# First group's 32 maxima and first row made inside the projections; the last batch's routing moved into the attention's first steps

## What is computed

```python
qkv = (x @ W_qkv + b_qkv).reshape(B, T, 3, H, Dh)          # 16 heads of 16
q, k = rope(q), rope(k)
attn = softmax(einsum('bhqd,bhkd->bhqk', q, k) / 4)         # 1024 x 1024 for each of 64 heads
out = einsum('bhqk,bhkd->bhqd', attn, v) @ W_out + b_out
scores = sigmoid(x @ w_gate.T)                              # 16 experts in 4 groups
# the 2 best groups by the sum of their two best scores, in them the 4 best experts,
# their scores normalised to weights; a shared gated network of 256 beside them
routed = einsum('tef,ehf,te->th', silu(x@w1_e) * (x@w3_e), w2_e, combine)
```

## Time and profile before

| | us |
|---|---|
| median of 3 runs | 1216.02 |
| profiled execution, span from first to last instruction | 1217.1 |
| PE busy | 1150.2 (95%) |
| DVE busy | 959.9 (79%) |
| ACT busy | 750.6 (62%) |
| POOL busy | 578.9 (48%) |
| L1048, maximum on DVE, x512 | 1.222 each |
| L1022, exponential on ACT, x1024 | 0.596 each |
| stage A | 0 to 158.7 |
| prologue of stage B | 158.7 to 198.4 |
| attention's steps | 198.4 to 845 |
| stages C and D | 845 to 1217 |

### The profile page before, as it was taken

How to read it: one execution, slowest core, us unless ns; L and a number is a source line. 1 busy time by engine, 2 the same in 40 slices (tenths; PEclk the granted TensorE clock), 3 DMA queues, 4 the chain that set the end, 5 groups by cost and what they waited for, 6 DMA issues and landing times. The chain is left out here.

```text
span 1217.1 us, 27786 instructions
## 1 busy us (share of the span) xinstructions
PE 1150.2 (95%) x8310; PEld 582.5 (48%) x8311; DVE 959.9 (79%) x1451; ACT 750.6 (62%) x1568; POOL 578.9 (48%) x861
## 2 busy tenths in 40 slices
PE   4999767999999999999999999998999999998998
PEld 2555422333333333333333333333788887875665
DVE  6575685999999999999999999970555555556888
ACT  3666303888888888888888888887333333330000
POOL 6999947354465653232322323231576666661000
PEclk9999955999999999999999999999999999999999
DMA  6466743454435453343324332402777666655765
GB/s 221 156 202 216 224 110 140 180 163 125 126 106 145 125 143 86 87 109 96 94 80 117 89 95 79 103 29 64 215 225 228 205 204 213 194 165 185 234 220 173
DMA packets 127288, 181.74 MB, mean 149 GB/s; under 512 B 41441, under 2 KB 88929, under 8 KB 125282
## 3 DMA queue, kind: packets, MB, share of 16 engines
q1 hardware_dynamic: 111842, 138.55, 39.6%
q0 software_dynamic: 15360, 42.04, 10.0%
HBM read 99.71 MB, written 80.81 MB: 148 GB/s over the span
## 5 line engine op out<-in xcount | busy, mean ns | idle before, releaser
L1048 DVE TENSOR_REDUCE mx<-pm 128x1 f32<-128x1024 f32 x512 | 620.6, 1222 | 31.4 <-PE pm L1098 30.6
L1022 ACT ACTIVATE pr<-pst 128x512 f32<-128x512 f32 x1024 | 556.6, 596 | 86.3 <-PE pst L1109 34.9
L1098 PE MATMUL pm<-kt,qt 48*128 48x512 f32 x1024 | 386.6, 461 | 13.4 <-DMA qt<-s_q 8.0
L1109 PE MATMUL pst<-qt,kt 50*128 50x512 f32 x1024 | 377.7, 449 | 6.5 <-DMA qt<-s_m 6.5
L1121 PE MATMUL po<-pr,vt 128*17 128x256 f32 x4096 | 322.9, 388 | 9.9 <-ACT osb L1032 9.6
L1098 PEld LDWEIGHTS pm<-kt,qt 48*128 48x128 f32 x1024 | 157.1, 192 | 237.5 <-DVE mx L1048 173.1
L1274 POOL DMA_INDIRECT s_y<-ys_c,slot_c x144 | 139.6, 969 | 85.7 <-issue 46.4
L1121 PEld LDWEIGHTS po<-pr,vt 128*17 128x17 f32 x4096 | 69.0, 95 | 198.9 <-issue 110.3
L1109 PEld LDWEIGHTS pst<-qt,kt 50*128 50x128 f32 x1024 | 152.8, 186 | 18.8 <-ACT pr L1022 10.9
L950 POOL DMA_INDIRECT s_xg<-p_rows,p_slot x128 | 125.2, 978 | 56.0 <-issue 29.8
L1354 PE MATMUL pd<-w13s,xt_c 128*128 x576 | 149.5, 382 | 0.4 <-ACT xt_c L1284 0.4
(11 more groups left out here) (188 smaller groups left out, 1169.5 us busy)
## 6 DMA issues: line engine op xcount, KB each, us to landing
xg<-s_xg SPq DMA_DIRECT2D x144, 128.5 KB
yg<-s_y SPq DMA_DIRECT2D x32, 512.0 KB, 3.9
s_q<-stg SPq DMA_DIRECT2D x32, 256.0 KB
s_k<-stg SPq DMA_DIRECT2D x32, 256.0 KB
kt<-s_k SPq DMA_DIRECT2D x32, 256.0 KB
qt<-s_q SPq DMA_DIRECT2D x64, 128.0 KB
s_o<-osb SPq DMA_DIRECT2D x32, 256.0 KB, 6.9
w13s<-w SPq DMA_DIRECT2D x1, 4608.0 KB, 14.6
```

Of the source, the lines that this page charges most:

```text
L1022: nc.scalar.activation(pr[:, (k % 2) * 4 + ORDER[i], :], pst[bank(gg, k, i)][:, :], ACT.Exp, scale=SCALE).then_inc(exp_ok, 1)
L1048: nc.vector.tensor_reduce(mx[:, half, col:col + 1], pm[slot][:, :, :].rearrange("p a n -> p (a n)"), AX.X, ALU.max).then_inc(mx_free, 1)
L1098: mm = pe.matmul(pm[slot][:, kk, :], qt[buf][rows, half, pair, qi * P:(qi + 1) * P], kt[buf][rows, pair, kk * 512:(kk + 1) * 512], start=T ...
L1109: pe.matmul(pst[bank(buf, k, i)][:, :], kt[buf][rows, pair, kc * P:(kc + 1) * P], qt[buf][rows, half, pair, :], start=True, stop=True)\
```

## The change

- The first group's keys and queries are loaded at step n = 15 of stage A (`FIRST_LOADS`), half 1 of the queries at 17, the values at 28; the second group's at n = 33 to 36.
- All 32 maxima of group 0 are made in stage A with one slot `pm0`, by a table `EARLY` of step and count: up to three in a step, on PE behind the turn back, behind the pQ matmuls, and behind the pV matmuls. To make room in PSUM, `pT` and `pV` have one buffer. The first row is split by POOL at n = 28, turned by DVE at 29, written by SP at 30 and read back at 31.
- The last batch's routing stands at the head of DVE's stream in stage B, behind a zeroing of `po`. Group 0 makes no maxima for k below 4.
- POOL's `choose` waits for that routing; the counting matmuls go into `pm0` at g = 0, k = 13 (COUNT), ACT's copies stand before that step's exponentials, and that step's maxima follow its scores. `number_choices` follows at k = 12's split, the planning comes two half groups later: `plan_counts` at g = 1, k = 11, `plan_tiles` at g = 2, k = 4, and the catching up of the scatter lasts until j = 3.
- On SP in stage B the second half's stores and w13 follow `rows(1, ...)` of group 0; the other weights are loaded in group 2.
- Stage A's loops are written out. Stage D waits on a semaphore for one product of stage C; `sg_d` shares its memory with the routing's buffers.

```diff
+FIRST_LOADS = 15
+EARLY = {17: 2, 18: 2, 19: 1, 20: 1, 21: 1, 22: 1, 23: 1, 24: 3, 25: 3, 26: 3, 27: 1, 28: 1, 29: 1, 30: 1, 31: 1,
+         32: 2, 33: 2, 34: 2, 35: 2, 36: 1}
+SPLIT_A, TURN_A, ROWS_A = 28, 29, 30
+
+def early_use(n, spot):
+    if spot >= EARLY.get(n, 0):
+        return None
+    return sum(count for at, count in EARLY.items() if at < n) + spot
...
 # stage_a, SP
-            def first_loads(k, t, b):
...
+            def first_loads(n):
+                if n == FIRST_LOADS:
                     for i in range(2):
                         sp.wait_ge(st_out[i], STORES * 16)
+                    load_keys(sp, s_k, first["kt"][0], 0, first["qk_in"][0])
+                    load_queries(sp, s_q, first["qt"][0], 0, 0, first["qk_in"][0])
+                if n == FIRST_LOADS + 2:
+                    load_queries(sp, s_q, first["qt"][0], 1, 0, first["late_in"][0])
...
+                first_loads(n)
+                if n == ROWS_A:
+                    store_rows(sp, s_m, first, 0, 0)
+                if n == ROWS_A + 1:
+                    load_rows_back(sp, s_m, first, 0, 0, 0)
...
 # stage_a, DVE
+            for n in range(NT + BACK):
+                t, b = n % TPB, n // TPB
+                if n < NT:
+                    other_stats(n, t, b)
+                early(n, 0)
+                if n >= BACK:
+                    rest(n - BACK, (n - BACK) % TPB, (n - BACK) // TPB)
+                early(n, 1)
+                early(n, 2)
+                if TPB <= n < NT:
+                    routing(n - TPB, t, b - 1)
+                if n == TURN_A:
+                    turn_rows(nc, dve, first, 0, 0, 0)
...
 # stage_a, PE
+            def early(n, spot):
+                use = early_use(n, spot)
+                if use is None:
+                    return
+                if use == 0:
+                    pe.wait_ge(first["qk_in"][0], LOAD)
+                if use == 16:
+                    pe.wait_ge(first["late_in"][0], LATE)
+                for kk in range(2):
+                    max_half(pe, first, 0, use, 0, use, kk, use)
+
+            for n in range(NT + BACK):
+                if n >= BACK:
+                    back(n - BACK, (n - BACK) % TPB, (n - BACK) // TPB)
+                early(n, 0)
+                if 0 <= n - TURN < NT:
+                    turn(n - TURN, (n - TURN) % TPB, (n - TURN) // TPB)
+                k = n - PROJ
+                if 0 <= k < NT:
+                    project(k, k % TPB, k // TPB)
+                early(n, 1)
+                if 0 <= k < NT:
+                    project_v(k, k % TPB, k // TPB)
+                early(n, 2)
...
 # stage_b
-            if final(g) and k >= SWITCH:
+            if final(g) and k >= SWITCH or isinstance(g, int) and g == 0 and k < SWITCH:
                 return []
...
 # stage_b, SP
-            load_keys(sp, s_k, kt[1], 1, qk_in[1])
-            load_queries(sp, s_q, qt[1], 0, 1, qk_in[1])
-            load_queries(sp, s_q, qt[1], 1, 1, late_in[1])
-            load_v(1, 0, 1)
             store_half(sp, s_q, s_k, first["stg"], B - 1, 0, first["st_out"][0])
-            rows(0, 0, 0)
-            store_half(sp, s_q, s_k, first["stg"], B - 1, 1, first["st_out"][1])
...
                     rows(2 * g + 1, 1, gg)
-                    if isinstance(g, int) and g < 2:
-                        weights(g)
+                    if isinstance(g, int) and g == 0:
+                        store_half(sp, s_q, s_k, first["stg"], B - 1, 1, first["st_out"][1])
+                        weights(0)
...
                     if not final(g):
                         rows(2 * g + 2, 0, 1 - gg)
+                    if isinstance(g, int) and g == 2:
+                        weights(1)
...
 # stage_b, POOL
-            split(0, 0, 15)
-            number_choices(nc, planned, plan, keep, ws_ok)
+            split(1, 1, 31)
+            wait_alone(pool, route_ok, 1, passed)
+            choose(nc, planned, plan, keep, sel_ok)
             plan_counters(nc, planned, plan, counters_ok)
...
 # stage_b, DVE
+            nc.vector.memset(po[:, :], 0.0).then_inc(po_ok, 1)
+            routed = Chain(dve, first["dve_own"])
+            routed.base = first["setup"] + ROOT_LINKS + (B - 1) * ROUTE_LINKS
+            for piece in range(5):
+                route(nc, dve, routed, first["gb"], keep, B - 1, piece, first["ex_ok"], first["ex_used"], keep["passed_dve"])
+            dve.sem_inc(route_ok, 1)
...
 # stage_b, PE
+            def counts(freed):
+                pe.wait_ge(sel_ok, 1)
+                need(pe, mx_free, freed)
+                pe.matmul(pm[0][:, 0, :], keep["ones"][:], sel, start=True, stop=True)
+                pe.matmul(pm[0][:, 1, :], keep["below"][:], sel, start=True, stop=True).then_inc(pre_ok, 1)
...
+                        if counting:
+                            pe.wait_ge(keep_ok, 2)
+                            for m in range(2):
+                                for kk in range(2):
+                                    max_half(pe, first, mbuf, us[m], m, place(g, k, m), kk, place(g, k, m) - 1)
```

More of the change, by code:

```diff
@@ L98, in rounds, with rounds_last @@
         emit(j)
-def rounds_last(eng, n, emit):
-    emit(0)
-    with eng.Fori(1, n - 1) as j:
+def rounds_last(eng, n, emit, head):
+    for j in range(head):
+        emit(j)
+    with eng.Fori(head, n - 1) as j:
         emit(j)
@@ L292, in sines @@
                 nc.gpsimd.tensor_tensor(qr[:, sl, :], rc[:, sl, :], rs[:, sl, :], ALU.add).then_inc(qr_ok, 1)
-            steps(pool, B, TPB, NT, [(PROJ, sines)])
+            for n in range(NT + PROJ):
+                if n >= PROJ:
+                    sines(n - PROJ, (n - PROJ) % TPB, (n - PROJ) // TPB)
+                if n == SPLIT_A:
+                    pool.wait_ge(mx_free, 16)
+                    split_maxima(nc, own, first, 0, mp_ok)
         @block.vector
@@ L340, in _ @@
             setup = own.n
+            first["setup"] = setup
             def other_stats(k, t, b):
[L344 removed]
+                if b:
                     return
@@ L375, in routing @@
                 assert t != TPB - 1 or own.n == ROUTE_LINKS, own.n
-            steps(dve, B, TPB, NT, [(0, other_stats), (BACK, rest), (TPB, routing)])
+            def early(n, spot):
+                use = early_use(n, spot)
+                if use is not None:
+                    row_maximum(nc, dve, first, use, 0, use)
+            for n in range(NT + BACK):
[11 more added lines that the diff above has]
+                    turn_rows(nc, dve, first, 0, 0, 0)
         @block.scalar
@@ L491, with max_half @@
 STORES = 4 * PARTS
+FIRST_LOADS = 15
[6 more added lines that the diff above has]
+    return sum(count for at, count in EARLY.items() if at < n) + spot
+def max_half(pe, first, buf, task, slot, use, kk, freed):
+    half, par, pair, qi = place_of(task)
+    if kk == 0:
+        need(pe, first["mx_free"], freed)
+    rows = slice(par * LANE, par * LANE + KR)
+    mm = pe.matmul(first["pm"][slot][:, kk, :], first["qt"][buf][rows, half, pair, qi * P:(qi + 1) * P],
+                   first["kt"][buf][rows, pair, kk * 512:(kk + 1) * 512], start=True, stop=True)
+    if kk == 1:
+        mm.then_inc(first["mx_full"], 1)
@@ L494, with load_rows_back @@
+def load_rows_back(sp, s_m, first, n, half, buf):
+    sp.wait_ge(first["mt_out"], 16 * (n + 1))
+    for par in range(2):
+        at, w = par * LANE + KR, 8 * PARTS
+        turned = s_m[half].rearrange("(b j) i -> j b i", b=4)[par * w:(par + 1) * w, :, :]
+        sp.dma_start(first["qt"][buf][at:at + MR, half, :, :].rearrange("p a q -> p (a q)").bitcast(F32), turned)\
+            .then_inc(first["mrow_in"][half], 16)
 PAD = 8
@@ L1003, in body @@
                             send(*tile)
-            for j in range(3):
+            for j in range(4):
                 body(j)
-            with pool.Fori(3, NG // 2 - 1) as j:
+            with pool.Fori(4, NG // 2 - 1) as j:
                 body(j)
@@ L1018, in body @@
                         q = g * QUADS + k
+                        if isinstance(g, int) and g == 0 and k == COUNT:
+                            act.wait_ge(pre_ok, 1)
+                            for kk, (name, done) in enumerate((("tiles", keep_ok), ("pre", keep_ok))):
+                                nc.scalar.activation(keep[name][:].rearrange("p n e -> p (n e)"), pm[0][:, kk, :], ACT.Copy)\
+                                    .then_inc(done, 1)
                         need(act, pv_ok, 2 * (q - 1))
```

290 lines of the change are left out of this document (141 added, 149 removed).

## The result

The changed kernel takes 1258.01 us (median of 4, 1250.70 to 1265.90) against 1216.15: a ratio of 1.0345, 95% interval 1.0316 to 1.0374. Forecast were 1233.5 us and a range of 1209 to 1241. The direction was right; the forecast rise, 17.5 us, was less than half of the measured 41.9. The profiled execution took 1250.7 us, its span is 1249.1. In e5 to e12 every kernel, the one before too, was slower (1386 us in place of 1216). Their traces show why only in part: from some 330 us on PE, DVE and ACT stop together for 2 to 5 us, some 25 to 30 us apart (in e10 all three first from about 340 to 343 us; e13's trace has none of it), and the granted clock is 0.50 behind many of these pauses. What stops them is open. So those runs are read by their traces up to there and by their ratio, which leaves out executions over 1.5% above their kernel's fastest (e7's rests on three of ten).

The account below looks back on a forecast made before the run. Projections were held bound by PE, as full as POOL, with 39.7 us without scores behind them. Terms -3.6 (first score), +1.3 (group 0), +12.1 (row), +6.4 (clock), +1.3 (plan_counts) gave +17.5: 1233.5 us, range 1209 to 1241.

Parts of the forecast that it names:

- part 1: Projections with 32 maxima: PE waits 12.7 us for first keys and queries; first score at 194.8, 3.6 us earlier.
- parts 2, 3: Group 0: last batch's routing on DVE costs nothing, or 1 us at full clock; counts at k=13 cost 2.6 us.
- part 3: Counting step, group 0, k=13: DVE empty a half step, PE makes maxima without a score; 2.6 us, from 1.2 to 2.9.
- part 4: SP's queue: w13 behind the stores, group 1's row behind w13; PE waits 12.1 us, low clock costs 6.4.
- S': Time of the attention's first score after the change, forecast 194.8 us, range 188 to 200.
- small transfers passing large ones: Rival, start of group 1: s_m is written beside w13, the row lands before S'+46.5; 1213.0 us, chance 0.19.
- maxima taken out of the attention's first four steps give nothing there: Group 0's first steps: a half step without maxima costs the same, so removing them there wins no time.
- low longer: Clock rival, start of attention: half clock lasts longer without maxima, row wait takes most up; 1235; no separate chance.
- the sum ends with plan_counts in group 1: Last term: plan_counts moves from group 0 to group 1, +1.3 us; no term for later groups.
- the sum moves both alike: Whole kernel: the same +17.5 us applied to profiled span (1217.1 to 1234.6) and median (1216.0 to 1233.5).

Follow-up runs that it names:

- e5: The change with w13 loaded in group 1 and w2, w_out, b_out in group 2, behind the second half's row loads: 1402.82 us, ratio 1.0116 to the kernel before.
- e12: The change with later weights, planning at step 2 of group 2, and eight maxima back in group 0's first steps with routing pieces behind them: ratio 0.9982.
- e10: The change with later weights (w13 in group 1, w2 in group 2) and tile planning at step 2 of group 2: ratio 1.0066 to the kernel before.
- e13: Repeat of e11 (later weights, planning at step 2 of group 2, unread products in group 0's first steps): 1225.89 us, ratio 1.0100.
- e7: The change with later weights, first maxima at step 22 of the projections and tile planning at step 2 of group 2: ratio 0.9948 to the kernel before.
- e6: The change with the first maxima at step 22 of the projections in place of 17, all 32 still made there: 1403.39 us, ratio 1.016.
- e14: As e13, but with the first maxima at step 20 of the projections: 1220.66 us, ratio 1.0046 to the kernel before.
- e1: The change with w2, w_out and b_out loaded in group 1, no longer in front of group 4's keys: 1245.0 us, ratio 1.0254.
- e4: The change with four 512-column products that nobody reads in each of steps 0 to 3 of group 0: 1260.53 us, ratio 1.0372.
- e9: The change itself measured again, unaltered, against the kernel before: ratio 1.0225.
- e15: The change itself measured again, on one chip with e13 and e14: 1257.19 us, ratio 1.0344 to the kernel before.
- e3: The change with the VectorE tile planning at step 2 of group 2 in place of step 4: 1253.2 us, ratio 1.0319.
- e11: As e10, plus four 512-column products that nobody reads in each of steps 0 to 3 of group 0: ratio 1.0044.

## Why the prediction was wrong

**The first loads (part 1): right in kind, low in size.** PE's first maximum came at 89.69 and not 84, the wait was 17.2 and not 12.7 (bounds 82 to 87 too early). The mis-sized piece is the landing: SP's last issue ended at 82.31 (forecast 81.7), the data were there 7.4 us later and not 2.3. The projections behind made up 4.0 of the 5.7 us: first score at 196.5 against 194.8. A later start does not win the wait back (e6, e14).

**Counting and routing (parts 2, 3): held.** Routing ran on DVE from 197.02 to 204.67 under group 0. The counting step left DVE idle for 3.14 us and PE for 1.31, put at 2.6 together; e5 shows that it can cost a stretch of clock too, which part 3 did not charge.

**The row behind w13 (part 4): right, nearly to the microsecond.** w13 at S'+36.6 (forecast 35.3), the read 21.1 us behind it (20.5), landed 2.8 later (2.8). The wait was 5.5 and not 12.1, only because group 1 came to it 8.5 us later than reckoned (251.5, S'+55.0). The bound on the other side, small transfers passing large ones, did not occur: s_m, issued at 241.71, was over only at 254.19. In the eight profiled executions with w13 ahead of that row (the change, e1 to e4, e6, e9, e15) s_m was issued anywhere from 3.5 to 17.1 us behind w13, and the read that waits for it went out 20.9 to 21.6 us behind w13 each time. The Trainium skill (DMA: Bandwidth & Descriptors, Queues, rings and completion order) says that completion does not follow the order of issue. No trace here has this small transfer done ahead of w13.

**The first step that failed: "maxima taken out of the attention's first four steps give nothing there".** By length they give nothing, by clock they cost 7.1 us in this execution (-1.9 at the first score to +5.2 at unit 0), 2.6 to 6.2 in eight others. The forecast had "low longer" as a rival at 1235, on the ground that the row wait would take it up; it did, and row wait, clock and counting from the first score to unit 1 made 16.7 us, forecast 19.8. So this alone did not break the number.

**The step that did: the sum ends with plan_counts in group 1, and the rest of the attention was put at nothing, without a reason.** It cost 15.0 us (4.7 + 10.3), which would have made the forecast 1248.5. Two things were left out that the diff shows. weights(1) moved from behind the rows of group 1's second half to the end of group 2, right before group 4's keys on the same queue: +10.3. The VectorE planning at step 4 of group 2 released a POOL chain whose 1.81 us fill stood before the split of the maxima that DVE wanted in that same step: +4.7. Part 4 followed one reordering of SP's queue and stopped there. In the profiled run's own terms, the forecast's 17.5 and then for each stretch the measured less the forecast: 17.5 + 1.7 (first score) - 3.1 (first score to unit 1) + 1.3 (unit 1 to 2, half clock behind the row wait) - 0.4 (unit 2 to 3, plan_counts: 0.9 for 1.3) + 4.7 + 10.3 = 32.0, the span's difference. e1 took away the key wait, e3 the stall of step 4 and e5 both waits behind weights. e11 and e13 stand within 1 us of the kernel before at unit 4, but as a balance: a first score 2.8 and 2.9 us earlier than before and, in e13, the 3.3 us that the products gain pay for the counting step. So the places are shown one by one, and the size of each varies by execution.

**The other failed step: "the sum moves both alike".** The profiled execution of the change was its fastest; the median is 7.3 us over it (1258.0 against 1250.7), where before the profiled span alone lay 1.1 above the median, and a time is 1.4 to 1.7 us more than its span in the executions that have both. These two explain the 9.9 us from the 32.0 of the profiles to the 41.9 of the medians. The change's spans, 1249.1 to 1264.3, go with the clock, 0.963 to 0.951; span times clock is 1199.0 to 1202.9. In e15's six it is 1199.6 to 1204.2, while the time spans 20 us. So there the executions seem to do the same work and to lose a different amount to stretches at half clock. The spread was 15 and 20 us for the change, 1.2 to 6.6 for the kernel before. That its new waits make the spread is argued and not shown: e13, with one of them left, still spread by 14 us. By medians, e13 leaves 10.7 of 42 us: that rest is in executions that were not profiled (their clock 0.968 to 0.982, their time 1219.4 to 1232.6; the profiled one's 0.981 and 1218.5), perhaps clock behind the 17.9 us wait, as in e10, or a short wait like e14's in group 3; where it lies is open.

## What to carry to other kernels

Where a change reorders a queue, list every transfer on it again with what is due behind it, up to the end of the last group it touches: here a term that took two lines of the diff was a third of the loss in the profiled execution (10.3 of 32.0 us). On a PE-bound stretch price a wait as itself and the half clock behind it (3.1 us here behind 1.6 us of waiting, 3.5 behind 6.8; in the other executions with the key wait 2.5 to 6.1), and compare the profiled execution with the median before trusting its sum. Work that costs no time because it runs beside other work may still be what holds the clock up.

## What the runs showed that was not expected

PE was hardly idle, and at half clock for 32 us: from 196.5 to 228.5 it was busy 31.7 of 32.0 us. The first step with maxima began at 211.3, and the clock rose 17 us behind it, in e1 with the same instructions there already at 217. With four more products in each of the first four steps the same stretch lasted 10.7 us (e4), 14 (e11) and 6 (e13). The length differs between executions of nearly the same instructions elsewhere too: behind a wait of 17 to 18 us in the projections the clock was back at 94 to 101 us, once at 115 (e10).

The kernel before stands at 0.50 through most of 151 to 214 us. Up to its first score at 198.4 PE waits there for DVE's maxima and for two transfers (8.0 and 6.3 us), so the half clock can cost it little; no run tried full clock there. The mean granted clock of e13's profiled run is higher than that of the kernel before (0.981 against 0.972) at the same span: a higher mean clock is no shorter time.
